# Attention slots: value projection and its bias ahead of the first maxima products, second scores and second maxima products ahead of the first values

## The reference

```
q, k, v = heads(x @ Wq + bq), heads(x @ Wk + bk), heads(x @ Wv + bv)
scores  = einsum('bhsd,bhtd->bhst', q, k) * SCALE
ctx     = einsum('bhst,bhtd->bhsd', softmax(scores), v)
output  = merge(ctx) @ Wo + bo
```

## Time and profile before

| | |
|---|---|
| median of 3 runs | 583.49 us (583.43 to 586.56) |
| the profiled execution's own time | 586.48 us |
| its span, first to last instruction | 583.8 us |
| TensorE busy | 517.5 us, 89% |
| VectorE busy | 453.7 us, 78% |
| ScalarE busy | 333.0 us, 57% |
| GpSimd busy | 218.5 us, 37% |
| mean granted TensorE clock | 0.970 |

### The profile page before, as it was taken

How to read it: one execution, slowest core, us unless ns; L and a number is a source line. 1 busy time by engine, 2 the same in 40 slices (tenths; PEclk the granted TensorE clock), 3 DMA queues, 4 the chain that set the end, 5 groups by cost and what they waited for, 6 DMA issues and landing times.

```text
span 583.8 us, 14064 instructions
## 1 busy us (share of the span) xinstructions
PE 517.5 (89%) x5230; PEld 283.9 (49%) x5230; DVE 453.7 (78%) x1021; ACT 333.0 (57%) x578; POOL 218.5 (37%) x333
## 2 busy tenths in 40 slices
PE   2788888899999999999998888879999989897975
PEld 1355563233333333333334555554444469797864
DVE  4577768789998998998974787958777679977567
ACT  3256666477787778778776666550112065457541
POOL 7113301702112421330243525065145278966243
PEclk9989999699999999999999999999999999999678
DMA  4456520230002203030312134045865600010001
GB/s 126 105 135 163 147 67 2 56 97 2 20 3 74 68 8 96 2 98 15 78 36 56 44 89 111 4 136 167 279 224 164 212 1 2 8 40 11 0 20 54
DMA packets 48302, 44.04 MB, mean 75 GB/s; under 512 B 7206, under 2 KB 39206, under 8 KB 48230
## 3 DMA queue, kind: packets, MB, share of 16 engines
q1 hardware_dynamic: 46220, 42.40, 25.1%
q10 hardware_dynamic: 2016, 0.75, 0.5%
HBM read 25.18 MB, written 1.18 MB: 45 GB/s over the span
## 4 chain that ended last, share of the span: by engine, by line
PE 66%; DVE 11%; ACT 9%; issue 5%; POOL 4%; DMA 3%; ACTq 1%; SPq 1%; DVEq 0%; POOLq 0%
PE banks L1224 13%; PE banks L1204 8%; PE banks L1139 5%; PE banks L569 5%; ACT probs L733 5%; PE banks L1849 5%; PE banks L469 5%; PE banks L552 3%; DMA past_mem<-gates 2%; PE banks L1235 2%; DVE negmax L884 2%; PE banks L2649 2%; DVE rec_negmax L1453 1%; PE banks L526 1%; DVE shared L1972 1%
## 5 line engine op out<-in xcount | busy, mean ns | idle before, releaser
L1453 DVE TENSOR_REDUCE rec_negmax<-banks 128x2 bf16<-128x512 f32 x256 | 165.2, 687 | 23.3 <-PE banks L1139 21.1
L1346 ACT ACTIVATE probs<-banks 128x1024 f32<-128x1024 f32 x128 | 131.1, 1025 | 47.8 <-PE banks L1204 46.9
L884 DVE TENSOR_REDUCE negmax<-banks 128x8 bf16<-128x1024 f32 x64 | 78.2, 1222 | 31.7 <-PE banks L526 31.6
L1139 PE MATMUL banks<-shared 62*128 62x512 bf16 x256 | 96.6, 395 | 4.5 <-DVE rec_negmax L1453 4.1
L1204 PE MATMUL banks<-shared 64*128 64x256 bf16 x512 | 97.5, 278 | 0.0
L1224 PE MATMUL banks<-probs,past_mem 128*32 128x256 f32 x1024 | 83.1, 396 | 1.3 <-ACT o_T L1353 1.3
L733 ACT ACTIVATE probs<-banks 128x1024 f32<-128x1024 f32 x64 | 65.5, 1024 | 31.5 <-PE banks L552 31.0
L1204 PEld LDWEIGHTS banks<-shared 64*128 64x128 bf16 x512 | 30.1, 94 | 69.6 <-issue 65.0
L1849 PE MATMUL banks<-shared,w_r 128*128 128x512 f32 x128 | 59.6, 601 | 2.6 <-DVE shared L1972 2.5
L569 PE MATMUL banks<-probs,shared 128*32 128x128 f32 x1024 | 41.7, 281 | 19.6 <-ACT probs L733 19.3
L1972 DVE TENSOR_TENSOR shared<-past_mem,out_T 128x512 f32<-128x512 f32 x64 | 42.9, 690 | 14.0 <-DMA past_mem<-gates 11.5
(11 more groups left out here) (260 smaller groups left out, 980.6 us busy)
## 6 DMA issues: line engine op xcount, KB each, us to landing
past_mem<-gates SPq DMA_DIRECT2D x64, 256.0 KB, 4.6
shared<-qk_parts SPq DMA_DIRECT2D x84, 128.0 KB, 2.7
shared<-past_mem SPq DMA_DIRECT2D x30, 128.0 KB, 2.9
shared<-qk_parts SPq DMA_DIRECT2D x18, 64.0 KB, 2.1
shared<-rec_neg_T SPq DMA_DIRECT2D x64, 2.0 KB
Y<-in_x SPq DMA_DIRECT2D x4, 256.0 KB, 3.1
xk_T<-in_ctx_T SPq DMA_DIRECT2D x4, 256.0 KB, 3.4
w_r<-in_w_r SPq DMA_DIRECT2D x4, 256.0 KB, 3.4
```

Source lines behind the costliest of these rows:

```text
L884: nc.vector.tensor_reduce(c.negmax[:, i % 2, :].rearrange("p (r j) -> p r j", r=2)[:, :, 4 * half:4 * half + 4], c.max_pair.rearrange("p ( ...
L1139: self.nc.tensor.matmul(c.max_banks[r], c.QT[64 * r:64 * r + 62, g % 2, j, off:off + P], c.rKT[64 * r:64 * r + 62, j, :], start=True, stop ...
L1346: nc.scalar.activation(c.probs[:, i % 4, :], c.score_pairs[i % 2], ACT.Exp, scale=HEAD_SCALE)\
L1453: self.nc.vector.tensor_reduce(out, c.max_banks[r].rearrange("p (a t) -> p a t", a=NP_PAST), AX_X, ALU.max, negate=True).then_inc(s["rec_m ...
```

## The change

It moves steps within a slot and fits three waits to the new order; no operation is added or taken away.

1. TensorE: `project_v(t)` moves from behind `turn_norm` to a place between the first scores and the first maxima products.
2. TensorE: `scores(t-2, 1)` and `max_scores(t, 1)` move ahead of `values(t-2, 0)`.
3. VectorE: `add_v_bias(t)` moves from behind the second maximum to the head of the slot, ahead of the first maximum.
4. `project_v(i)` now waits for the normalisation of i-4 (in cross-attention from i = 5 on for the residual addition of i-5), and `turn_ctx(i)` for the bias of sequence i+3 in place of i+2, which is the bias of the same slot.

```diff
@@ project_v
-        if i >= 3:
-            pe.wait_ge(*s.after(ph + "norm", i - 2))
+        if cross and i >= 5:
+            pe.wait_ge(*s.after("cross_out", i - 4))
+        elif i >= 4:
+            pe.wait_ge(*s.after(ph + "norm", i - 3))
         elif i:
             pe.wait_ge(*s.after(ph + "v", i))
@@ turn_ctx
-        if i + 3 <= B:
-            pe.wait_ge(*s.after(ph + "v", i + 3))
+        if i + 4 <= B:
+            pe.wait_ge(*s.after(ph + "v", i + 4))
         else:
             pe.wait_ge(*s.after(ph + "norm", i))
@@ slot(t) of TensorE
         if t < B:
+            project_v(t)
             max_scores(t, 0)
...
         if 0 <= t - 2 < B:
-            values(t - 2, 0)
             scores(t - 2, 1)
         if not cross and t == 2:
             window(1)
...
             max_scores(t, 1)
         elif lead:
             lead(t, 1)
+        if 0 <= t - 2 < B:
+            values(t - 2, 0)
         if 0 <= t - 3 < B:
             turn_norm(t - 3)
         if lead and t == B:
             lead(t, 4)
         if cross and 0 <= t - 4 < B:
             cross_out(t - 4)
-        if t < B:
-            project_v(t)
@@ slot(t) of VectorE
         if t < B:
+            add_v_bias(t)
             maximum(t, 0)
...
             maximum(t, 1)
-            add_v_bias(t)
```

## The result

The changed kernel took 591.34 us in the median (588.91 to 596.33, 4 runs) against 583.46 us (583.41 to 586.56, 4 runs): ratio 1.0141, 95% interval [1.0094, 1.0189]. It is slower by 1.4%.

The account below looks back on a forecast made before the run. It took VectorE's chain from first maximum to window remainder to set the end of slots waiting for L422. Terms 2.2 + 0.4 + 0.24 + 0.24 + 1.1 - 1.2 - 0.6 + 0.15 = +2.5 us: 583.49 to 586.0, range 580.0 to 591.5.

Parts of the forecast that it names:

- What set the second exponential: In slots with ScalarE window work, its DMA issue, not the second scores: start stays 2.81, 0.61 behind the issue.
- The faster rival: If the 0.61 is a late signal of the second scores, some 19 slots gain about 0.4: 575.9 us, chance 0.10.
- What sets the end of the L422 slots: VectorE's first maximum to window remainder; window product follows 0.15 behind, second values 1.02 behind that.
- The step that failed: At TensorE's slot head, the projection holds some 0.23, moving the first maxima products from 0.23 to 0.46.
- 0.24: Delay of VectorE's first maximum in a slot; nine slots that wait for L422 make +2.2 us.
- the walk: Step-by-step timing of one self slot that waits for L422, after the change: from 4.82 to 5.06 us.
- The last slots: Self 17, cross 16 and 17, without maxima or projection: wait for the first maximum gone, 3 x -0.4 = -1.2 us.
- The slots outside L422: Self 8 and 12: 2 x +0.2; self 13: +0.24; self 4 and 14: 2 x +0.12 us.
- V1 comes out of its cover: First values uncovered, 0.4 in 28 slots: 594.7 us, chance 0.10; sign: 5.2 us or more outside L422 slots.
- Cross slots: Some 8 with little window work or with routing work: +0.14 each, +1.1 us; cross 2 and 12: 2 x -0.3.
- The clock rival: One more TensorE half-clock stretch of 10.24 us, about +4.9 on top of +2.5: 590.9 us, chance 0.10.
- The chances: Whole kernel: forecast 0.60, with nothing moving 0.70 for within 1%; faster 0.10, slower 0.20.

Follow-up runs that it names:

- e6: On top of e3, ScalarE's issue of the row DMA moved behind the second exponential: 582.79 us, one run.
- e3: Kernel before, with only the second scores moved ahead of the first values: 583.14 us, ratio 0.9987.
- e9: e7 plus e6's row DMA issue behind the second exponential, and second scores ahead of first values only in slots without maxima: 582.83 us, ratio 1.0012.
- e5: Changed kernel with each value projection computed twice into the same place, bias behind the second: 597.21 us, one run.
- e1: Kernel before, with only the value projection and its bias moved to the head of the slot: 592.70 us, ratio 1.0155.
- e2: Kernel before, with only the second scores and second maxima products moved ahead of the first values: 581.36 us, ratio 0.9952.
- e4: The changed kernel measured once more, against the kernel before: 592.30 us, ratio 1.0148.
- e7: Kernel before, with the value projection in self slots moved behind the turn of the context, bias late as before: 582.55 us, ratio 0.9977.
- e8: e7 plus, in self slots, remainder L422 ahead of the normalisation and window product ahead of the turned context: 582.83 us, ratio 1.0006.
- e12: e7 with e3's order in every slot and e6's row DMA issue behind the second exponential: 582.46 us, ratio 0.9978.

## Why the prediction was wrong, point by point

*What set the second exponential: right.* ScalarE's issue, not the second scores. The distance stayed at 2.36 to 2.40 in the ten self slots named, after as before, fell from 2.09 to 1.80 or 1.81 in self 4, 13 and 14, and e6 took it from e3's 2.37 to 1.64 by moving the issue alone. The second scores were the next limit, 0.28 earlier, as the prediction's 2.53 against 2.81 has it: with the issue moved and the scores late it is 2.09 (e9). The faster rival fell with it.

*What sets the end of the L422 slots: right.* First maximum, remainder, window product, second values. The chain came in its order and with its distances (the 0.15 ahead of the window product, the 1.02 behind it).

*The step that failed:* "The projection (0.39, holding TensorE some 0.23, as S1 does before M1) stands before M1: M1 goes from 0.23 to 0.46". It went to 0.75. I took the hold of a bfloat16 group for that of a float32 product between two bfloat16 groups; e5 shows 0.22 for the product and 0.30 for the place. With 0.52 for 0.24 the walk gives 5.34 for the L422 slots; 5.34 to 5.35 was measured in seven profiled self slots. In the sum that term becomes 9 x 0.52 = 4.7 instead of 2.2.

The same step has VectorE's side wrong. The bias was put at 0.67 and started at 0.85, and 0.67 + 0.28 is 0.95, not the 0.91 from which the 0.24 was taken. Even with the maxima products at 0.46 the first maximum would have been about 0.4 late (the estimate under e5), not 0.24.

One term explains nearly the whole miss. The 0.24 stands, openly or not, in 22 slots of the sum: 9 with L422, self 8 and 12, self 13, self 4 and 14, and the 8 cross slots. 22 x 0.28 more is 6.2, and 2.5 + 6.2 = 8.7 us, against the measured 7.9 and 8.8. This is worked out after the fact, and so close a match is partly luck: cross slots 2 and 12, put at -0.6 together, grew by 0.15, and the ten other cross slots up to 15 grew by 3.1 where this reckoning gives eight of them 3.4. The last slots gained 1.3 us where 1.2 was forecast, but not as forecast: self 16 0.41, cross 16 0.27, cross 17 0.58, and self 17, which was named, nothing in the end (its second values came 0.57 earlier, at 3.95 instead of 4.53, but the past attention's first products behind them wait for VectorE and are done no earlier).

*The slots outside L422:* "2 x +0.2" for self 8 and 12. They grew by 0.50 each (4.60 and 4.63 to 5.10 and 5.14); self 4 and 14, at +0.12 each, grew by 0.50 too, and self 13, at +0.24, by 0.52. e1 gives self 8 and 12 0.1, e2 0.2. Together it is more than the sum, because the second maxima products wait for the first maximum (until 2.47; 1.94 in e2) with the first values behind them: these start at 2.80 instead of 1.52. The walk had them at 2.52 and the second values of self 8 at 4.2; they came at 2.80 and 4.49, both 0.28 later, so this is the same step failing once more. It is also the rival "V1 comes out of its cover" in part. Its mechanism was real, its point of decision too (in L422 slots, where the window product stands later, it cost nothing), and the prediction's own sign of it, 5.2 us or more outside the L422 slots, came in cross slot 8 (5.32; e1 4.92, e2 5.03). Alone, as in e2, it costs the whole kernel nothing.

*Cross slots:* slots 2 to 16 grew by 4.0 us where the terms of the sum give about +0.6 (2 x 0.24 + 1.1, less 0.6 for slots 2 and 12 and 0.4 for slot 16). The same 0.5 appears in slots 3, 5, 7, 8 and 9 (5.47 to 5.95, 4.82 to 5.34, 4.40 to 4.90, 4.82 to 5.32, 4.83 to 5.35), and 0.25 to 0.32 in 4, 6, 10, 11 and 13; slot 16 gained 0.27, slot 2 nothing. Slot 14, with routing work on VectorE, grew by only 0.03.

*The clock rival:* no. The granted clock was 1.00 from 29 to 97 us with most slots 0.5 us longer, and in e4 the same. The rule cited from the Trainium skill ("TensorE: Matmul & The Clock Gate", "A second HAM failure mode: psum-queue depth-cycling") allows it to fall there; this trace shows that it didn't. It did fall for 3.4 us in the self slots of other orders: in slots 3 and 14 of e1, in slot 16 of e7 and e8, and in slot 3 of the kernel before. The stretch in e1's slot 14 made that slot 6.00 us long, where self 4 with the same steps took 4.69.

*The chances:* 0.70 within 1% rested on a term that I bounded from one side only. The delay of the first maximum was taken as a single value, 0.24, without an upper bound from the rows. The rows at hand would have given a larger one, though not the whole 0.52: in the earlier trace rows the projection takes 0.39, and a float32 product behind a bfloat16 group (the turn of the context behind the first maxima products) starts 0.32 behind it, not 0.23.

## What to carry to other kernels

Price a moved product by what stands before and behind it in its new place, not by its duration in the old one: a short float32 product dropped between two bfloat16 groups cost 0.52 us, and behind another float32 product, in a gap, nothing. Before bringing a step forward ask whose wait it really ends; an idle time put down to the last releaser may belong to the step ahead in the engine's own queue, such as the issue of a DMA. And two reorderings that cost 0.1 and 0.2 us in a slot cost 0.5 together, when one delays what the other has begun to wait for.

## What the runs showed of the hardware that I had not expected

*The place of a float32 product.* Between bfloat16 groups the value projection costs 0.30 us beside its own 0.22 (e5). Of this, 0.10 is the way in, and it isn't the projection's alone: the first values (e3, e12) and the turn of the context also start 0.32 to 0.33 behind a bfloat16 group, where another bfloat16 group starts 0.23 behind. The 0.20 of the way out is not general: behind the sixteen float32 products of the first values a bfloat16 group starts after 0.58 and a float32 product after 0.58 too (e12 and the profile after). What makes either of them (the weight loads that can't be taken ahead, or the change of type itself) no run here separates; that stays open.

*A DMA issue on ScalarE* holds its queue for about 0.6 us but not the engine: issued behind an exponential it ran beside it (e6). The Trainium skill, "DMA: Bandwidth & Descriptors", section "Issuing engines are not separate DMA queues", calls the sequencer's time to start a DMA usually small relative to the DMA; here it was 0.51 us by the row, and 0.61 to the next exponential.

*TensorE's clock outside the loops* goes with much of the difference between spans, which differ more than the slots do. The stretch between the self slots' end and cross slot 2, by the windows view, of before, after, and the changed kernel again (e4):

```profile
98.05:313.76 215.71, 208.59 (x2071) 74.39 (x2068) 185.58 (x329) 161.72 (x213) 60.90 (x99) 0.98 0.17 44
```
```profile
102.85:317.14 214.29, 207.89 (x2070) 74.49 (x2067) 185.52 (x329) 161.65 (x213) 60.74 (x99) 0.98 0.17 45
```
```profile
104.65:318.05 213.40, 206.68 (x2070) 74.44 (x2067) 185.20 (x329) 161.84 (x213) 60.88 (x99) 0.99 0.17 45
```

The half-clock time near 105 to 120 us was 10.2, 6.8 and 3.4 us in them. It was also 3.4 us in e2 (213.41 us for this stretch) and 10.2 in e7 and e8 (215.5 us each). Such a stretch comes and goes with the execution, so single runs of one kernel spread (35 runs of the kernel before: 578.85 to 589.85 us), and a gain like that of e2, which the loops don't show, may be one of where the stretches fall. Over its whole span the profile of e2 has about 28 us at half clock and that of before about 35. One execution of e2 took 779.69 us, at a mean granted clock of 0.568; it has no profile, and what held the clock down stays open. Whether the order of the last self slots has a part in where the stretches fall was not tried.
